# Audio tower kernel with 32 experts: the experts' products and outputs three and four iterations behind their gathers instead of two and three

## The reference

```python
Sm = softmax(xf @ W_router + b_router)
G_ek, idx_ek = top_k(Sm.T, k)              # k = 16*742//32 = 371 tokens for each expert
tokens = xf[idx_ek]
up = einsum('gjkh,ghf->gjkf', tok_g, W_up) + b_up      # 8 groups of 4 experts share W_up
act = silu(up)
Eout = einsum('ekf,efh->ekh', act, W_down) + b_down
y = zeros.at[idx_ek].add(G_ek[..., None] * Eout)
```

## Time and profile before

| | us |
|---|---|
| median of 3 runs | 913.53 |
| lowest and highest | 909.73, 915.24 |
| the profiled execution | 913.51 |
| its span, first to last instruction | 911.7 |

### The profile page before, as it was taken

The page is one execution under the profiler, slowest core; times in us unless marked ns, Lnnn a source line. Parts: engine busy times, 40 slices in busy tenths (PEclk is TensorE's granted clock), DMA queues, the critical chain, the costliest instruction groups (busy, mean ns, idle before and its releaser), DMA issues. The chain is left out here.

```text
span 911.7 us, 22856 instructions
## 1 busy us (share of the span) xinstructions
PE 773.9 (85%) x7417; PEld 604.6 (66%) x7417; DVE 646.9 (71%) x2345; ACT 527.2 (58%) x1161; POOL 400.9 (44%) x434
## 2 busy tenths in 40 slices
PE   7999999999999999999998446786877877799872
PEld 5687778777877787778866334565655655587661
DVE  4568888898889888988897676777777777723210
ACT  2667768767876687777765452655545545523220
POOL 6122322133213322232122201576688787868784
PEclk9999999999999999999999655877999899889996
DMA  5001202211121102120210201233343334434332
GB/s 119 2 2 46 66 24 67 62 47 39 48 65 44 56 31 65 43 65 22 65 43 23 79 1 50 50 58 62 51 76 60 63 63 74 67 54 77 61 44 20
DMA packets 66497, 46.77 MB, mean 51 GB/s; under 512 B 9760, under 2 KB 62688, under 8 KB 66432
## 3 DMA queue, kind: packets, MB, share of 16 engines
q1 hardware_dynamic: 46976, 32.21, 12.2%
q0 software_dynamic: 19456, 13.74, 11.0%
HBM read 25.69 MB, written 20.23 MB: 50 GB/s over the span
## 5 line engine op out<-in xcount | busy, mean ns | idle before, releaser
L652 POOL DMA_INDIRECT out_dram<-tqk,idx x96 | 154.3, 1608 | 55.0 <-issue 27.8
L642 POOL DMA_INDIRECT f<-token_rows,idx x96 | 96.6, 1006 | 48.7 <-issue 43.4
L590 POOL TENSOR_TENSOR wnorm<-wnorm,expo 128x6 f32<-128x6 f32 x16 | 21.2, 1324 | 200.3 <-DVE wnorm L1225 172.9
L879 PE MATMUL pa<-wc,xT 128*128 128x128 f32 x768 | 101.6, 275 | 1.3 <-ACT kt L725 0.8
L879 PEld LDWEIGHTS pa<-wc,xT 128*128 128x128 f32 x768 | 93.5, 192 | 2.0 <-issue 2.0
L1101 PE MATMUL po<-qb 114*128 114x128 f32 (+1 forms) x576 | 88.2, 320 | 0.8 <-ACT qb L824 0.8
L1101 PEld LDWEIGHTS po<-qb 114*128 114x128 f32 (+1 forms) x576 | 82.9, 228 | 1.5 <-issue 1.4
L947 PE MATMUL pst<-sv,kt 128*128 128x136 f32 x352 | 76.9, 300 | 8.1 <-DVE state L1326 7.4
L947 PEld LDWEIGHTS pst<-sv,kt 128*128 128x128 f32 x352 | 55.6, 191 | 27.4 <-DVE state L1326 15.2
L1312 DVE TENSOR_TENSOR P<-scores,causal 128x512 f32<-128x512 f32 x96 | 65.9, 687 | 4.7 <-PE scores L934 2.8
L735 ACT ACTIVATE qb<-f,turn_of 128x384 f32<-128x384 f32 x128 | 67.8, 601 | 0.0
(11 more groups left out here) (273 smaller groups left out, 1950.5 us busy)
## 6 DMA issues: line engine op xcount, KB each, us to landing
token_rows<-row SPq DMA_DIRECT2D x16, 480.0 KB, 3.0
xT<-in_x_cols_dram SPq DMA_DIRECT2D x17, 388.0 KB, 3.5
out_dram<-h SPq DMA_DIRECT2D x16, 384.0 KB, 3.0
qb<-in_L_ffn_W_down_dram SPq DMA_DIRECT2D x32, 171.0 KB
xr<-in_x_rows_dram SPq DMA_DIRECT2D x17, 192.0 KB, 3.4
f<-token_rows,idx POOLq DMA_INDIRECT x96
out_dram<-tqk,idx POOLq DMA_INDIRECT x96
spare<-in_L_ffn_W_up_dram SPq DMA_DIRECT2D x8, 170.5 KB
```

The lines of the kernel that those rows point to most:

```text
L642: eng.indirect_dma_start(out=xg[0:n, e.par, t, :], out_offset=None, in_=rows[:, :], in_offset=bass.IndirectOffsetOnAxis(ap=idx[0:n, e.slot ...
L652: eng.indirect_dma_start(out=out_rows, out_offset=bass.IndirectOffsetOnAxis(ap=idx[0:n, e.slot, t:t + 1], axis=0), in_=yw[0:n, e.par, t, : ...
L879: eng.matmul(dst, xT[:, b.par, a:a + C], wc[:, t, :], start=(t == 0), stop=False)
```

## The change

F lags three iterations instead of two, and D four instead of three. There is a third row buffer, in another quarter of tile f, with a semaphore x_got of its own; the buffer goes by the expert's number modulo 3. The indices have eight buffers, one for each k, and the wait that guards them goes back to expert e-8. The waits that free a row buffer go from two experts back to three. Group 0's rounds are spread 0, 0, 2, 2, 3, 3, 3, 3 over its iterations instead of 0, 0, 1, 3, 3, 3, 3, 3. Two more things follow from BEHIND: the drain has four iterations instead of three, and two small pairs of keep-busy products stand beside experts 0 to 2 instead of 0 and 1. In iteration 2 neither F nor D has an expert.

```diff
-        idx = sb("idx", [SL, 4, 3], i32)
-
-        xg = f[0:SL, :, :, :].rearrange("p a w t -> p a (w t)")[:, :, 0:3 * ROW].rearrange("p a (t d) -> p a t d", t=3)
+        idx = sb("idx", [SL, EG, 3], i32)
+
+        xg = [f[0:SL, a, w, 0:3 * ROW].rearrange("p (t d) -> p t d", t=3) for a, w in ((0, 0), (1, 0), (1, 1))]
...
-        x_got = [sem("x_got0"), sem("x_got1")]
+        x_got = [sem("x_got0"), sem("x_got1"), sem("x_got2")]
...
+            def third(self):
+                return self.index() % 3
...
-        BEHIND = {"I": 0, "Q": 0, "F": 2, "D": 3}
+        BEHIND = {"I": 0, "Q": 0, "F": 3, "D": 4}
...
-        TURNS_OF = [[0, 0, 1, 3, 3, 3, 3, 3], [2] * EG, [2] * EG]
+        TURNS_OF = [[0, 0, 2, 2, 3, 3, 3, 3], [2] * EG, [2] * EG]
...
-                    hold(eng, "xgt_ps", e.count(1, 1, back=2))
-                    hold(eng, "gcol_done", e.count(2, 2, back=2))
+                    hold(eng, "xgt_ps", e.count(1, 1, back=3))
+                    hold(eng, "gcol_done", e.count(2, 2, back=3))
                     for t in range(3):
                         n = GOT[t]
                         eng.indirect_dma_start(
-                            out=xg[0:n, e.par, t, :], out_offset=None, in_=rows[:, :],
-                            in_offset=bass.IndirectOffsetOnAxis(ap=idx[0:n, e.slot, t:t + 1], axis=0)
-                        ).then_inc(x_got[e.par], 16)
+                            out=xg[e.third()][0:n, t, :], out_offset=None, in_=rows[:, :],
+                            in_offset=bass.IndirectOffsetOnAxis(ap=idx[0:n, e.k, t:t + 1], axis=0)
+                        ).then_inc(x_got[e.third()], 16)
...
-                            out=out_rows, out_offset=bass.IndirectOffsetOnAxis(ap=idx[0:n, e.slot, t:t + 1], axis=0),
+                            out=out_rows, out_offset=bass.IndirectOffsetOnAxis(ap=idx[0:n, e.k, t:t + 1], axis=0),
...
-                    need(eng, x_got[e.par], e.half() * 48)
+                    need(eng, x_got[e.third()], (e.index() // 3 + 1) * 48)
...
-                        mm = eng.transpose(p_xg[:, SLOT0[t]:SLOT0[t] + n], xg[0:n, e.par, t, 0:D], ident[0:n, 0:n])
+                        mm = eng.transpose(p_xg[:, SLOT0[t]:SLOT0[t] + n], xg[e.third()][0:n, t, 0:D], ident[0:n, 0:n])
...
-                    need(eng, y_out, e.count(48, 0, back=3))
+                    need(eng, y_out, e.count(48, 0, back=EG - 1))
...
-                    eng.scalar_tensor_tensor(out=idx[:, e.slot, :], in0=p_small[0:SL, 4:7], scalar=-float(C), in1=wrap[:, :],
+                    eng.scalar_tensor_tensor(out=idx[:, e.k, :], in0=p_small[0:SL, 4:7], scalar=-float(C), in1=wrap[:, :],
```

More of the change, by code:

```diff
@@ L1568, in part2 @@
                 if (stage, what) == ("F", "x"):
-                    need(eng, x_got[e.par], e.half() * 48)
+                    need(eng, x_got[e.third()], (e.index() // 3 + 1) * 48)
                     need(eng, "yw_done", e.count(2, 2, back=2))
                     own = bass.ds(e.index() + D, 1)
-                    eng.tensor_copy(gcol[:, e.par, 0:2].unsqueeze(2), xg[:, e.par, 0:2, own]).then_inc(S["gcol_done"], 1)
+                    eng.tensor_copy(gcol[:, e.par, 0:2].unsqueeze(2), xg[e.third()][:, 0:2, own]).then_inc(S["gcol_done"], 1)
                     n = PUT[2]
-                    eng.tensor_copy(gcol[0:n, e.par, 2:3], xg[0:n, e.par, 2, own]).then_inc(S["gcol_done"], 1)
+                    eng.tensor_copy(gcol[0:n, e.par, 2:3], xg[e.third()][0:n, 2, own]).then_inc(S["gcol_done"], 1)
                 if (stage, what) == ("I", "cnt"):
```

## The result

| | before | after |
|---|---|---|
| median of this comparison's runs, us | 914.38 (909.73 to 916.73, 4 runs) | 925.47 (923.46 to 926.96, 4 runs) |
| profiled execution / its span, us | 913.51 / 911.7 | 924.77 / 923.0 |
| ratio to before | 1 | 1.0124 (1.0091 to 1.0157) |

The changed kernel is 1.2% slower, 11.1 us; 6.7 us were forecast. On a second chip the same two kernels stood at 916.09 and 909.15 us, 1.0079 (1.0054 to 1.0104), 6.9 us. The first lies inside the range given by 0.5 us only, and outside the 917 to 923 of the forecast itself; the second, as a ratio, lies inside both. Which side of 1% the truth is on, the two comparisons leave open.

A forecast was written before the change was run, and what follows sets the result against it. POOL was taken to set the pace in group 3 and the drain, the search's chain DVE, ACT, PE before that. Terms +7.9 - 0.4 - 0.8 = +6.7 on 913.51 gave 920.2 us, range 912 to 926.

The forecast's parts named there:

- Part 1: Behind the last gather: four scatters instead of three, the one missing early being hidden in group 0; +7.9 us.
- Part 2: Gathers' slack: none late in groups 0 to 2, and group 3's POOL already without gaps; 0, at most 3.8 us won.
- rival (d): Gathers secretly late in groups 0 to 2: 3.8 us plus 10.5 of boundary waits won, 905.9 us; chance 0.05.
- Part 3: Group boundaries: POOL's waits of 4.60, 3.01 and 3.80 us for an old expert's product stay; 0, bound -10.5.
- rival (a): Group boundaries: the third buffer lets the others get ahead and POOL's waits are absorbed, 10.5 us less, 909.7 us; chance 0.10.
- Part 4: Group 0: iterations 2 and 3 take 18.5 us against 18.88, -0.4; the four later ones 44.0 against 44.83, -0.8.
- rival (b): Group 0: PE, little used in iteration 2, runs the next iterations at the lower clock, 924.6 us; chance 0.20.
- Part 5: Buffers: third row buffer and W_down's reload cost nothing, eight index buffers remove a harmless wait; 0, bound 0.8 us.

The follow-up runs named there:

- e3: The changed kernel with one more iteration of lag, F four and D five behind, and a fourth row buffer: 918.04 us, 1.0155 of before.
- e5: The changed kernel brought back to lags 2 and 3 from iteration 26, in group 3, by an extra pass of F and D: 918.15 us, 1.012 of before.
- e2: The kernel before with only the new spread of group 0's rounds, lags 2 and 3 kept: 902.54 us, 0.999 of before.
- e4: The changed kernel with 2 in place of 10 keep-busy products ahead of the first expert's transposes: 909.59 us, 1.0069 of before.
- e10: The changed kernel brought back to lags 2 and 3 from iteration 5, with 2 in place of 10 first keep-busy products: 921.36 us, 1.0098 of before.
- e7: The kernel before with eight index buffers and the guarding wait on expert e-8's scatter in place of e-4's: 909.06 us, 1.001 of before.
- c2: The changed kernel, unaltered, run on chip 8 beside the kernel before: 916.09 us, 1.0079 of before.
- e9: The kernel before with 2 in place of 10 keep-busy products ahead of the first expert's transposes: 914.8 us, 0.9991 of before.
- e8: The kernel before without most loads of W_up and W_down, later experts computing with old weights: 913.44 us, 0.9997 of before.

## Why the prediction was right, and where it was not

**Part 1, +7.9: right, measured +8.5 to +8.8.** Four scatters behind the last gather, one more landing each, linear in the lag (e3), and moved but not removed by e5. The surplus of the first pair, 0.9, is 0.4 in the three steps (24.10 us in sum for three of 7.90) and 0.5 in the last expert (12.26 us from 910.74 to the span's end, 11.73 from 899.97 in before).

**Part 2, 0: right here.** From 637 to 884 us no wait for a gather is left among the changed kernel's waits; group 3's 14.4 us of DVE are gone and POOL's eight experts there take 77.20 us for 78.13, 0.9 less, about what a gap of 1.12 us at 864.83 in before took beyond the usual 0.30. At 740.80 the transposes start 16.9 us after the last issue of their gather at 723.87, where the earlier trace rows had 3.36; I had said some 10 us ahead, and the slower boundary iteration adds the rest. On chip 11 the gathers were late in groups 1 and 2, rival (d)'s condition, and 1.4 us lie between e2 and e4, one execution each, less than the 3.8 that I allowed, since POOL was within 3.0 us of its least.

**Part 3, 0: right in kind.** The boundary waits stay, 2.2 us shorter, 9.17 us in sum for 11.41, and four waits of 1.67 to 2.45 us for the same product stand elsewhere in groups 1 and 2, where before had none that long. In the kernels of chip 11 the second and third of these waits are gone with lags 2 and 3 too (e2), so it isn't the lag that absorbed them: rival (a)'s effect occurs there without rival (a)'s cause.

**Part 4: the mis-sized term.** Iterations 2 and 3 were forecast at 18.5 us, -0.4; they took 21.53, +2.65 (on chip 8 21.62, +1.5). Of the 3.0 us above the forecast 0.5 is iteration 2 and 2.6 iteration 3. The step that failed is "bounded above by 10.0 (a full two-round iteration", said of iteration 3: the first expert's F carries ten keep-busy products where a later one has four, and I had these in hand, since my own working of iteration 2 put its wait of 2.38 us down to them. I took the wait away from iteration 2 and did not put it down in iteration 3. e4 and e10 measure it at 1.7 to 2.1 us; the rest I put down to the lower clock, which no run shows by itself. e2 adds that the same ten products and two rounds in iteration 2, at the old lag, cost as much: the loss goes with the two rounds behind them, at either lag. The part of the clock is rival (b)'s mechanism, in one iteration and not in the four later: those ran at 0.81 and took 44.00 us, as forecast, not 48. By the rule of "TensorE: Matmul & The Clock Gate" in the Trainium skill, that activity releases the throttled state, iteration 2 was the weak place; the trace agrees, with 0.50 there for 0.86 in before. But most of the miss did not reach the end: the boundary's wait shrank from 4.60 to 3.15 us. Counted from the end of iteration 1, its scatter came 0.1 us earlier than before (74.54 us for 74.61) where part 4 as forecast gives 1.2, and 0.2 later on chip 8.

**Part 5, 0: right** (e7).

**Sum.** Ahead of iteration 2 -0.7 (chance, the change doesn't touch it), from there to the boundary -0.1 (forecast -1.2), the end +8.8 (forecast +7.9), which is 921.5; the remaining 3.3 us are in the 24 experts, where I forecast 0. In the traces they are in group 1: its seven iterations took 4.5 us more, at a granted clock of 0.91 for 0.98, while group 2's took 1.3 less and group 3's eight experts 0.9 less. A cause in the change isn't shown, since the same instructions differ by 6.8 us between c2 and e5. On chip 8 the medians are 6.9 us apart, less than the drain alone. On the first chip 11.1 us do leave some 3, and whether these are chance or the change, no run settles.

So the direction and the largest term were forecast with their mechanism, and the total in part by luck. The 925.47 us lie beside rival (b)'s 924.6, but (b)'s four slow iterations did not come; and chip 8's +6.9 lies beside the forecast's +6.7 though the end alone is +8.5 there.

## To carry to other kernels

A pipeline stage made one iteration later pays its own tail once at the end, bare: before counting the slack that it gives, find the last instruction of the queue that bounds the kernel and see what follows it. Slack given to a queue that is served by a full engine (here POOL, at 9.64 us per expert) shows as waits that vanish from the others, 16.5 us of them, and as almost no time. When a step moves into another iteration, count its preparations there too: every warm-up product ahead of it is queued ahead of whatever else is now in that iteration.

## What was not expected

- Ten warm-up products meant to help cost 1.7 to 2.1 us with two search rounds in their iteration, and nothing that shows with one (e9): mostly at the lower level 24 passes took 4.85 us, and 8 took 1.14 at the upper.
- The same work of seven iterations took from 58.4 to 75 us among kernels that differ little, and the same instructions took 164.3 and 157.5 us on one chip (c2, e5). It isn't the weight loads (e8). It goes with PE's granted clock; at both lags on chip 8 there are short and long ones, and chip 11's two shortest are of kernels with the longer lags.
- Chip 11 ran the kernel before in 903.6 us, chip 8 in 909.15 and 913.96 in two comparisons: differences of the size of the effect studied, so that kernels can be compared only with a kernel before that ran beside them.
